# Attention block with expert layer on one core: three images per VectorE multiply, and gates scaled by a reciprocal deviation kept in rows

## What is computed

```python
x = x + conv_block(_ln_c(x))          # layer norm over the 32 channels, then window attention
t = tokens(x)                          # 8 x 4096 tokens of 32 channels
t = t + ffn(_ln_t(t))                  # layer norm over the 32 channels of a token, then experts
# conv_block: per-image, per-channel norm over the pixels; 1x1 q, k, v; attention of 4 heads in
#   8 x 8 windows (softmax over 64 keys); 1x1 projection
# ffn: router_probs = softmax(t @ router_w + router_b)        # 8 experts
#      top_p, top_i = top_k(router_probs, 2); top_p /= sum(top_p)
#      out = sum over the two of top_p * (t @ expert_w[i] + expert_b[i])
```

## Time and profile before

| | us |
|---|---|
| median of 3 runs | 372.4 (371.52 to 372.99) |
| the profiled execution | 372.87 |
| its span | 371.0 |

### The profile page before, as it was taken

How to read it: one execution, slowest core, us unless ns; L and a number is a source line. 1 busy time by engine, 2 the same in 40 slices (tenths; PEclk the granted TensorE clock), 3 DMA queues, 4 the chain that set the end, 5 groups by cost and what they waited for, 6 DMA issues and landing times.

```text
span 371.0 us, 12911 instructions
## 1 busy us (share of the span) xinstructions
PE 333.5 (90%) x5496; PEld 176.2 (47%) x5496; DVE 321.3 (87%) x421; ACT 276.8 (75%) x481; POOL 165.4 (45%) x192
## 2 busy tenths in 40 slices
PE   8999888999999979999989989989988997878885
PEld 2556466566566545556555655556542221121221
DVE  1599989998998987999998896899897999999884
ACT  4678768879879885788778897876766788466762
POOL 8520000220220223578535212378658658764663
PEclk9999999999999998999999999999989999687999
DMA  8800010010010000100101101075320856673582
GB/s 299 346 4 3 3 32 11 23 30 18 16 33 29 4 27 7 30 24 10 32 2 31 33 2 32 23 178 117 67 49 29 197 123 129 151 169 86 127 207 96
DMA packets 13386, 26.19 MB, mean 71 GB/s; under 512 B 1681, under 2 KB 3857, under 8 KB 12945
## 3 DMA queue, kind: packets, MB, share of 16 engines
q1 hardware_dynamic: 12752, 23.60, 24.3%
q10 hardware_dynamic: 576, 1.77, 1.2%
HBM read 5.96 MB, written 4.19 MB: 27 GB/s over the span
## 4 chain that ended last, share of the span: by engine, by line
PE 50%; DVE 26%; issue 9%; ACT 8%; DMA 4%; POOL 2%; SPq 0%; POOLq 0%; DVEq 0%; ACTq 0%
PE psum L694 12%; PE psum L713 7%; DVE neg_max L1321 6%; PE psum L679 6%; PE psum L721 4%; PE psum L874 4%; DVE window_work L1324 4%; PE psum L663 4%; PE psum L597 3%; DMA stage<-in_x 2%; DVE window_work L1469 2%; DVE o_tok L1332 2%; DVE probs L1469 2%; PE psum L492 2%; PE psum L864 2%
## 5 line engine op out<-in xcount | busy, mean ns | idle before, releaser
L370 POOL TENSOR_TENSOR o_norm<-o_tok,o_rden 128x128 f32<-128x128 f32 x64 | 24.7, 407 | 155.7 <-DVE o_rden L1334 155.7
L1023 ACT ACTIVATE probs<-psum 128x512 f32<-128x512 f32 x128 | 74.9, 597 | 24.6 <-PE psum L694 23.9
L694 PE MATMUL psum<-weights_sb,window_work 128*128 128x128 f32 x512 | 80.2, 283 | 6.2 <-ACT probs L1023 3.4
L1321 DVE TENSOR_REDUCE neg_max<-psum 128x16 f32<-128x1024 f32 x64 | 76.8, 1199 | 6.3 <-PE psum L679 6.3
L1324 DVE TENSOR_TENSOR window_work<-psum,neg_max 128x1024 f32<-128x1024 f32 x64 | 78.4, 1225 | 2.2
L694 PEld LDWEIGHTS psum<-weights_sb,window_work 128*128 128x128 f32 x512 | 54.7, 140 | 36.8 <-issue 17.5
L713 PE MATMUL psum<-probs,v_cols 128*32 128x64 f32 x2048 | 49.7, 226 | 0.3 <-DVE o_tok L1332 0.3
L713 PEld LDWEIGHTS psum<-probs,v_cols 128*32 128x32 f32 x2048 | 33.7, 111 | 27.8 <-ACT probs L1023 14.1
L1006 ACT ACTIVATE stage<-k_sb,weights_sb 128x512 f32<-128x512 f32 x64 | 44.3, 724 | 0.0
L679 PE MATMUL psum<-stage 32*64 32x256 f32 x1024 | 35.9, 386 | 8.8 <-DVE window_work L1324 6.1
L1332 DVE STREAM_TRANSPOSE o_tok<-psum 128x512 f32<-128x512 f32 x32 | 22.8, 712 | 13.6 <-PE psum L713 13.6
(11 more groups left out here) (148 smaller groups left out, 609.0 us busy)
## 6 DMA issues: line engine op xcount, KB each, us to landing
stage<-act_all SPq DMA_DIRECT2D x36, 256.0 KB, 4.3
out<-v_cols SPq DMA_DIRECT2D x16, 256.0 KB, 2.0
stage<-in_x SPq DMA_DIRECT2D x3, 1024.0 KB, 12.9
x_moved<-x_cur SPq DMA_DIRECT2D x14, 192.0 KB, 2.4
gate_rows<-gate_parts SPq DMA_DIRECT2D x16, 128.0 KB, 3.0
x_moved<-x_cur SPq DMA_DIRECT2D x14, 64.0 KB, 2.2
weights_sb<-weights ACTq DMA_DIRECT2D x1, 811.5 KB, 13.4
stage<-in_x SPq DMA_DIRECT2D x1, 768.0 KB, 5.7
```

The source lines that it names most:

```text
L694: last = nc.tensor.transpose(bank[TURN_BANKS[v % 2]][:, b * P:b * P + P], heads.rearrange("p h k -> p (h k)"), const["c_ident"][:, :])
L1023: nc.scalar.activation(probs[:, w % 4, :], bank[TURN_BANKS[w % 2]][:, :], ACT.Exp).then_inc(exp_done, 1)
L1321: nc.vector.tensor_reduce(m_t, t, AX.X, ALU.max, negate=True).then_inc(max_done, 1)
```

## The change

**Images.** In chunks 1 to 10 of the experts, 20 halves, DVE multiplies images 1 to 3 with banks 3 to 5 in one instruction of 128 x 1536 that waits for both gate pairs and raises `scaled_done` by two. In chunks 0 and 11 to 15 the two instructions stay.

**Deviation.** ACT computes `Ln(var + eps)` and then `Exp(-0.5 * that)`, the reciprocal deviation in rows, into `rstd_two`; the Exp is now step 0. The logits are raw logits times this (step 1) plus the bias (step 2, on POOL for quads 0 and 1, on ACT for quads 2 and 3). The transpose and the reciprocal of the deviation, the multiply of the gap and that of the best probability are gone. The gate matrix is turned into `gate_f32` (step 22), and step 23, on DVE, multiplies it by `rstd_two` for the splits; POOL's multiply L431 is gone. The list has 28 steps, and the tables are written anew.

```diff
-        GATE_OPS = 30
+        GATE_OPS = 28
...
-        LATE_POOL = {EARLY: (6, 14, 21, 22, 23, 27, 29),
-                     EARLY + 1: (6, 14, 21, 27)}
...
+        LATE_POOL = {EARLY: (6, 13, 19, 20, 21, 27),
+                     EARLY + 1: (6, 13, 19)}
...
-            EARLY_STEPS = (((), (2,)), ((5, 6), (8, 9)), ((11, 12, 13, 14), (16,)), ((21, 22, 23), (26, 27)), ((29,), ()))
+            EARLY_STEPS = (((), (1, 2)), ((5, 6), (8, 9)), ((11, 12, 13), (15,)), ((19, 20, 21), (25,)), ((27,), ()))
...
-                nc.scalar.activation(std_two[:, quad % 2, :], bank[SHARED][:, :], ACT.Sqrt,
+                nc.scalar.activation(rstd_two[:, quad % 2, :], bank[SHARED][:, :], ACT.Ln,
                                      bias=const["c_eps"][:, 1:2]).then_inc(ln2["std_ready"], 1)
+                act.wait_ge(ln2["std_ready"], quad + (1 + ONE))
+                nc.scalar.activation(rstd_two[:, quad % 2, :], rstd_two[:, quad % 2, :], ACT.Exp, scale=-0.5
+                                     ).then_inc(gate_step[quad], 1)
...
+                if step == 2:
+                    one = nc.scalar.activation(spaces[quad].logit, spaces[quad].logit, ACT.Identity,
+                                               bias=const["c_rb"][:, 0:1])
...
-                if n == 0:
-                    dve.wait_ge(ln2["std_ready"], quad + (1 + ONE))
-                    one = v.transpose(w.std_t, std_two[:, quad % 2, :])
-                elif n == 1:
-                    one = v.reciprocal(small[:, rden, :], g(w.std_t)[:, :, 0])
-                elif n == 2:
+                if n == 1:
                     dve.wait_ge(raw_done, quad + 1)
...
+                    one = v.tensor_tensor(w.logit, rstd_two[:, quad % 2, :], raw_logits[:, :], ALU.mult)
...
-                    one = v.transpose(w.rest, w.sum)
...
+                    one = v.transpose(gate_f32[:, quad % 2 * CHUNK:(quad % 2 + 1) * CHUNK], w.sum)
                 elif n == 23:
+                    one = v.tensor_tensor(w.rest, gate_f32[:, quad % 2 * CHUNK:(quad % 2 + 1) * CHUNK],
+                                          rstd_two[:, quad % 2, :], ALU.mult)
...
-            EARLY_STEPS = {(6, 8): (0, 1), (7, 8): (3, 4), (8, 1): (7,), (8, 8): (10,), (9, 1): (15,),
-                           (9, 8): (17, 18, 19, 20), (10, 1): (24,)}
+            EARLY_STEPS = {(7, 8): (3, 4), (8, 1): (7,), (8, 8): (10,), (9, 1): (14,), (9, 8): (16, 17, 18), (10, 1): (22, 23)}
...
+                    if 1 <= c <= 10:
+                        dve.wait_ge(gate_ps, c * 4 + (2 * eh + 2))
+                        nc.vector.tensor_tensor(scaled[eh][:, 1:4, :], x_rep[:, slot(c), 1:4, :], psum[:, 3:6, :],
+                                                ALU.mult).then_inc(scaled_done, 2)
```

More of the change, by code:

```diff
@@ L75, in metaformer_block @@
         std = std_pair[:, 0, :]
[L76 removed]
+        rstd_two = sb("rstd_two", [P, 2, CHUNK])
         raw_logits = sb("raw_logits", [P, CHUNK])
@@ L255, in __init__ @@
                 self.mask1 = at[3]
-                self.std_t, self.rest = std_pair[:, quad % 2, :], std_pair[:, quad % 2, :]
+                self.rest = std_pair[:, quad % 2, :]
         spaces = [Gates(quad) for quad in range(QUADS)]
-        best, second, best_rank, second_rank, gap, e_gap, total, p_best, p_second, rden, near = range(11)
+        best, second, best_rank, second_rank, gap, e_gap, total, p_best, p_second = range(9)
         rank8 = const["c_rank"][:, :].unsqueeze(1).to_broadcast([P, CHUNK // E, E])
@@ L398, in gates @@
                 w = spaces[quad]
[L399 removed]
+                if n == 1:
                     pool.wait_ge(raw_done, quad + 1)
[L401 to L402 removed]
+                    one = pool.tensor_tensor(w.logit, rstd_two[:, quad % 2, :], raw_logits[:, :], ALU.mult)
+                elif n == 2:
+                    one = pool.tensor_scalar(w.logit, w.logit, const["c_rb"][:, 0:1], None, ALU.add)
                 elif n == 5:
                     one = equal(g(w.a), g(w.logit_t), wide(best))
[L405 removed]
+                elif n in (6, 13):
                     one = pool.tensor_tensor(g(w.b), g(w.a), rank8, ALU.mult)
@@ L1382, in gates @@
                 elif n == 11:
-                    one = v.tensor_tensor(small[:, near, :], small[:, second, :], small[:, best, :], ALU.subtract)
+                    one = v.tensor_tensor(small[:, gap, :], small[:, second, :], small[:, best, :], ALU.subtract)
                 elif n == 12:
-                    one = v.tensor_tensor(small[:, gap, :], small[:, near, :], small[:, rden, :], ALU.mult)
-                elif n == 13:
                     one = v.tensor_tensor(g(w.a), g(w.rest), wide(second), ALU.is_equal)
+                elif n == 14:
+                    one = v.tensor_reduce(small[:, second_rank, :], g(w.b), AX.X, ALU.max)
@@ L1457, in steps @@
                     for n in late_steps(quad, 2 * c + eh):
-                        if n not in LATE_POOL[quad] and n not in (25, 28):
+                        if n not in LATE_POOL[quad] and n not in (2, 24, 26):
                             gates(quad, n)
```

93 lines of the change are left out of this document (36 added, 57 removed).

## The result

| | before | changed |
|---|---|---|
| median of 4 runs each, same chip (us) | 372.69 (371.52 to 374.10) | 379.19 (378.64 to 379.64) |
| ratio, 95% interval | | 1.0172 (1.0132 to 1.0212) |
| profiled execution (us) | 372.87 | 379.58 |
| its span (us) | 371.0 | 377.8 |

The account below looks back on a forecast made before the run. The prediction took the chain as mostly PE's in attention, leaving for ACT or DVE at gate work, with DVE mattering only in some expert halves. Terms summed to +5.3 on 372.87, 378.2; median 0.5 lower, 377.7 us; 8-in-10 range 373.0 to 380.6.

Parts of the forecast that it names:

- Term 1: Attention chunk 6: two more table loads and the Exp on ACT, covered by nothing, +3.3 us.
- Term 2: Behind chunk 6: PE's longer idle time brings a second stretch at 1.2 GHz, +1.0 us (0 to 1.5).
- Term 3: Attention chunk 9: DVE's last small gate step runs ahead of POOL's instruction instead of blocked beside it, -1.2 us.
- Term 4: Attention chunk 10: DVE's added step 23 delays PE's turn of unit 2, +0.7 us.
- Term 5: Attention chunks 12 and 15: fewer DVE steps against ACT's Exp, -0.3 us; the Exp delays PE's start, +0.5 us.
- Term 6: Expert halves 1 to 4: step 23 and a bias on ACT, less a dropped step and merged multiplies, +0.8 us.
- Term 7: Expert halves 4 to 10: merges bring nothing; one more load and the Exp ahead of quad 3's raw logits, +2.0 us.
- Term 8: Expert halves 11 to 21: merges -0.8, fewer gate steps -1.2, waits on ACT +0.5, clock falls unchanged; -1.5 us.
- The end: Expert chunks 11 to 15: called unchanged, 0 us.
- The first rival: Whole expert stage: DVE sets the pace, so halves 4 to 10 gain too; 372.6 us, down to 370.4; chance 0.2.
- The merged multiply empties DVE: Halves 12, 16 to 18 and 20: up to 0.5 us lost each, third clock fall +3, 380.7 us; chance 0.14.
- The loads aren't there: Attention chunk 6 and expert chunk 4: one table serves both functions, each 1.28 us shorter, 375.1 us; chance 0.03.

Follow-up runs that it names:

- e3: Kernel before, plus one tiny Ln in attention chunk 6 that forces two more table loads there: 377.6 us, ratio 1.0136.
- e2: Changed kernel with the two separate multiplies back in expert chunks 1 to 10, so new gates alone: 381.4 us, ratio 1.0221.
- e5: Changed kernel with quad 3's Exp and its load moved behind the next gate bank copy, so raw logits come first: 377.06 us, ratio 1.0098.
- e10: Changed kernel with the move of quad 3's gate rows issued one expert chunk later, behind chunk 13's repeated tokens: 381.26 us, ratio 1.0246.
- e11: Changed kernel with quad 3's step 1 (reciprocal deviation times raw logits) in expert half 11 instead of 10: 380.64 us, ratio 1.023.
- e1: Kernel before with only the merged multiplies in expert chunks 1 to 10, old gates kept: 373.2 us against 373.0, ratio 1.0012.
- e7: e4 with one table set holding exponential and logarithm loaded ahead of attention, two loads in all: 368.12 us, ratio 0.9868.
- e9: e7 with the two separate multiplies back instead of the merged ones: 370.45 us, ratio 0.9905.
- e8: Kernel before (old gates and multiplies) with deviations as Exp(0.5 Ln) and the one table set preloaded: 370.02 us, ratio 0.989.
- e4: Changed kernel with the images' deviation also as Exp(0.5 Ln), so chunk 6 has two loads instead of four: 374.97 us, ratio 1.0059.
- e12: e7 with the edits of e5, e11 and e10 together: 370.11 us, ratio 0.9922.

## Why the prediction came out

The direction and the main mechanism were right: loads and an Exp on a chain over ACT that nothing covers, and PE's clock behind it. The time (377.7 forecast, 379.19 measured) was near. Both large losses stand where the forecast put them, and none of the rivals happened. By its terms:

- **Term 1 (+3.3) right.** 8.05 us from the first load to the exponential, forecast 8.0, against 4.69: +3.36. Nothing covered it, and e3 shows that for the loads alone.
- **Term 2 (+1.0) right in kind, too large for this execution.** From the exponential to PE's next keys L640 it is 9.73 us instead of 8.07, but from there to the end of the 48 matmuls 1.91 instead of 3.40: +0.17, for the half clock came earlier instead of twice. In five of the six profiles of kernels with four loads there (e2, e3, e5, e10, e11 and the changed kernel; the last is the exception) the half clock lasted twice as long as in the kernel before. Those built on the changed kernel were 0.7 to 1.2 us later in chunk 8 than it, so 1.0 is about the usual price and the profiled execution had the small one.
- **Term 3 (-1.2) right:** -1.38, by the row of 0.27 us.
- **Term 4 (+0.7) wrong:** +0.03. I took the first wait (PE's for unit 2, which came, 0.70 us) as the loss of the chunk. DVE's wait of 0.69 us for PE at the next chunk, which takes it up, was in the trace of before. A delay must be followed to the next point where the delayed engine waits.
- **Term 5 (-0.3, +0.5) right:** -0.25 and +0.46. The maximum of chunk 13 stands 0.17 us behind its scores.
- **Term 6 (+0.8) wrong in sign:** -0.63. Step 23 took 0.84 us, as priced. But the stretch of half clock at 276 us of the kernel before didn't come, and gave 1.56. I had counted the falls of the clock in the later halves and not this one, and e1 shows that a fall in unchanged code may come or not. The merged multiplies, put at a gain here, cost most of their 0.77 us in these halves (e2).
- **Term 7 (+2.0) undersized:** +4.68. The load and the Exp cost 1.95 us, as forecast. What was missing is the clock behind PE's longer wait, 2.10 us, though I had priced just that in chunk 6 (term 2) and had written "the same two falls" for this stage. That price holds for half 11 only: as the half clock moved and wasn't added, halves 11 to 22 have less of it. I had also put the gate steps that moved there into "half 10's idle time". They fit only because PE was late: without the loads and at full clock they make half 11 2.5 us late by themselves (e7), of which 1.2 is left at half 15. Between halves 4 and 10 DVE starts another 0.54 us later, but the chain isn't DVE's there, and ACT's copies of gate bank 2 take 6.30 us from half 7 to 9 in both kernels (296.59 to 302.89 and 299.44 to 305.74). From half 9 to 11 the copies are 3.97 us later, the two parts of the loss.
- **Term 8 (-1.5) right:** -1.56 from half 11 to 22, which took 33.92 us instead of 35.48. How much of that is the merge alone stays open, since e1 found none and e2 and e9 some 2 us, and a part is the clock: I had assumed it unchanged, and its mean was 0.84 instead of 0.81.
- **The end (0)** cost 1.49 us. I had called these chunks unchanged because their code is. They begin with transfers queued behind gate rows, whose issue took 1.1 us longer. Since that varies among kernels with the same tail, I don't put it down to the change.

The first rival ("DVE sets the pace of the whole expert stage") would have had halves 4 to 10 shrink; they didn't. Its lower end was also summed wrongly: 370.4 takes the 1.5 us of term 8 off in full, though 0.8 of it is in the 377.7 already, so 371.2 was meant. The second ("The merged multiply empties DVE") wanted up to 0.5 us of waiting in five halves and a third fall of the clock. DVE stood idle 4.6 us in all ahead of the 20 merged multiplies, 1.91 of it in half 11, and the clock of halves 11 to 22 was higher than before. "The loads aren't there" did not happen by itself, and it was priced too low. It was put at 2.6 us below the forecast, and when e7 made it happen the kernel was 11.1 us faster. Ten loads went and not two. Those of chunks 6 and 12 came back at more than their length (5.69 us for four, 2.69 for two), those of chunk 15 for 0.7 of 2.6, and the mean granted clock was 0.983 instead of 0.973.

The misses are -0.7 (terms 1 and 2), -0.7 (4), -1.4 (6), +2.7 (7) and +1.5 (the end), with 0.4 from the start and -0.2 from the rest. They largely cancel (+1.5 is left), so much of the closeness of the total is luck.

## What to carry to other kernels

In this kernel a function that needed another table cost its loads at full length where ACT was on the path. PE's clock behind the longer idle time cost another 1.2 us in e3 and 2.1 us in half 10. Before replacing a function, look which sets are loaded and whether one loaded by hand serves all; here that was worth more, by the medians, than the rewritten gates and the merged multiplies together (3.9 us from the kernel before to e8, another 1.9 to e7). When a delay is priced, follow it to the next wait of the engine that it delays (it may end there), and put the same price of the clock on every place where the same idle time grows.

## What the runs showed of the hardware

- **The same code, two clocks.** The kernel before and e1 have the same attention stage and the same idle time of PE (1.82 and 1.86 us at 138 us). In one the granted clock was half from 139.7 to 143.1 us, in the other it stayed at 2.4 GHz, and 1.36 us were between them. The 17 executions of the kernel before that ran beside e1 had mean granted clocks from 0.966 to 0.986. A single pair of profiles can't tell a change of that size from such chance.
- **A gain ahead can be paid back by the clock.** In its profiled execution e4 entered the experts 4.4 us earlier than the changed kernel and ended 2.9 us earlier, with two more stretches at 1.2 GHz between 275 and 292 us. The median of its executions is 4.2 us lower, so this is what happened once and not a price.
- **A load is 1283 ns, with nothing to be seen around it.** That is the mean of the changed kernel's twelve, and the next ACTIVATE starts 0.01 to 0.02 us behind the load.
- **DVE beside POOL.** The multiply of 128 x 512 with two inputs in SBUF took 1.75 us beside POOL's and 0.68 without. It cost nothing in the changed kernel, where PE was late anyway, and set the start of half 11 once the loads were gone (1.70 us in e12).
- **The merged form costs what its columns cost.** 128 x 1536 took 1750 ns. In half 8 the next step starts 1.67 us behind its start (302.82 to 304.49), against 1.73 us for the two that it replaces in the earlier trace rows (300.56 to 302.29). In a row of DVE work nearly the whole fixed cost was overlapped already. From half 1 to 9 it cost 0.77 us, with PE waiting 0.8 us longer for DVE's multiplies (e2, e9).
